# Inverses by logarithm and exponential, eight-largest routing, and eight maxima steps ahead in a two-layer kernel

## Time and profile before

| | |
|---|---|
| median of three runs | 3710.39 us |
| profiled execution, its span | 3709.09 us, 3707.4 us |
| busy: TensorE, VectorE, ScalarE, GpSimd | 81%, 67%, 56%, 35% |
| mean granted TensorE clock | 0.906 |
| 655 to 721 us, with the first combining stage | VectorE busy 43.1 us, TensorE 14.3 |
| 721 to 798 us, with routing | VectorE busy 57.7 us, TensorE 10.6 |
| 1088 to 1630 us, with the second attention | TensorE 454.0, VectorE 401.6, ScalarE 317.4, GpSimd 297.3 |
| 1630 to 1691 us, with the second combining stage | VectorE busy 38.8 us, TensorE 8.6 |
| 1691 to 3707 us, transformer blocks and the end | TensorE 1827.7, VectorE 1302.2 |

### The profile page before, as it was taken

The page is one execution under the profiler, slowest core; times in us unless marked ns, Lnnn a source line. Parts: engine busy times, 40 slices in busy tenths (PEclk is TensorE's granted clock), DMA queues, the critical chain, the costliest instruction groups (busy, mean ns, idle before and its releaser), DMA issues. The chain is left out here.

```text
span 3707.4 us, 71470 instructions
## 1 busy us (share of the span) xinstructions
PE 2992.1 (81%) x22883; PEld 1620.1 (44%) x22883; DVE 2466.2 (67%) x4021; ACT 2083.8 (56%) x3805; POOL 1285.4 (35%) x1223
## 2 busy tenths in 40 slices
PE   2688887239738888845999999999999999999997
PEld 1332332113312223313665565566556556655653
DVE  6788888562347777765666666666666666666664
ACT  1477677112204666633666666666666666666664
POOL 0000000004323556624553354345435434544540
PEclk6588789569957999977999999999999999999998
DMA  5221121114231111232111111111111111111111
GB/s 197 84 85 55 62 73 60 56 45 108 67 38 30 35 34 34 37 68 99 38 54 31 49 54 31 42 45 51 34 49 49 35 42 45 49 31 53 38 35 42
DMA packets 195211, 200.31 MB, mean 54 GB/s; under 512 B 119077, under 2 KB 125877, under 8 KB 190090
## 3 DMA queue, kind: packets, MB, share of 16 engines
q1 hardware_dynamic: 193778, 195.46, 19.2%
q10 hardware_dynamic: 1080, 0.25, 0.0%
HBM read 99.84 MB, written 29.46 MB: 35 GB/s over the span
## 5 line engine op out<-in xcount | busy, mean ns | idle before, releaser
L2421 POOL TENSOR_TENSOR tr_t<-tr_t 128x512 f32<-128x512 f32 x384 | 489.7, 1275 | 683.5 <-DVE tr_t L2259 683.5
L2428 POOL TENSOR_TENSOR tr_nq<-tr_t,tr_rn 128x512 f32<-128x512 f32 x384 | 392.2, 1042 | 366.5 <-ACT tr_rn L2155 362.7
L1638 DVE TENSOR_REDUCE attn_mp<-attn_ps 128x1 f32<-128x512 f32 (+3 forms) x664 | 397.3, 656 | 146.4 <-PE attn_ps L1498 76.5
L2258 DVE TENSOR_TENSOR tr_t<-tr_ps,tr_tab 128x512 f32<-128x512 f32 x384 | 263.2, 685 | 241.1 <-ACT tr_sq L2129 241.1
L1957 PE MATMUL tr_ps<-tr_w,tr_xs 128*128 128x512 f32 x768 | 372.5, 607 | 25.0 <-DVE tr_xs L2292 21.8
L684 DVE TENSOR_REDUCE attn_mcol<-attn_ps 128x1 f32<-128x512 f32 x548 | 357.3, 681 | 50.2 <-PE attn_ps L529 40.4
L1600 ACT ACTIVATE attn_pr<-attn_ps 128x768 f32<-128x768 f32 (+2 forms) x352 | 294.9, 868 | 142.3 <-PE attn_ps L1521 140.0
L2143 ACT ACTIVATE tr_rd<-tr_ps 128x384 f32<-128x384 f32 x264 | 129.0, 489 | 376.1 <-PE tr_ps L1976 375.9
L1943 PEld LDWEIGHTS tr_ps<-tr_qT,tr_kT 64*128 64x128 f32 x4224 | 258.5, 188 | 176.6 <-issue 174.9
L1943 PE MATMUL tr_ps<-tr_qT,tr_kT 64*128 64x96 f32 (+1 forms) x4224 | 301.2, 282 | 31.4 <-ACT tr_kT L2164 20.1
L668 ACT ACTIVATE attn_pr<-attn_ps 128x512 f32<-128x512 f32 x512 | 272.6, 600 | 87.1 <-DVE attn_ps L706 68.9
(11 more groups left out here) (257 smaller groups left out, 5177.0 us busy)
## 6 DMA issues: line engine op xcount, KB each, us to landing
tr_v<-tr_va SPq DMA_DIRECT2D x144, 192.0 KB, 2.6
attn_ka<-scratch_kp SPq DMA_DIRECT2D x72, 294.0 KB
tr_v<-tr_va SPq DMA_DIRECT2D x144, 128.0 KB, 2.2
moe_cb<-scratch_combineT SPq DMA_DIRECT2D x32, 512.0 KB
tr_w<-in_w_half SPq DMA_DIRECT2D x12, 1024.0 KB
tr_v<-tr_va SPq DMA_DIRECT2D x48, 256.0 KB, 2.4
scratch_kp<-proj_parts SPq DMA_DIRECT2D x36, 256.0 KB
attn_km<-scratch_kp SPq DMA_DIRECT2D x72, 98.0 KB
```

What stands on the lines that cost most here:

```text
L1638: dve.tensor_reduce(dst, src, AX.X, ALU.max).then_inc(maxed, 1)
L2258: dve.tensor_tensor(out[0], product, table[0], ALU.mult)
L2421: pool.tensor_tensor(t12[:, slot, i, 0, :], t12[:, slot, i, 0, :], t12[:, slot, i, 1, :], ALU.add).then_inc(summed, 1)
L2428: pool.tensor_tensor(nq[:, slot, i, :].rearrange("p (h e) -> p h e", e=DH), t12[:, slot, i, 0, :].rearrange("p (h e) -> p h e", e=DH), rn[ ...
```

## The change

In both combining stages ScalarE makes the softmax inverses, as exp(-ln(den)), one batch entry at a time; the table set that holds both functions is loaded at the stage's start. The sigmoid of the gate becomes an exponential on ScalarE and an addition and a small reciprocal on VectorE. The loads are put in order of batch entry, and VectorE and TensorE go by chunks or batch entries in place of the whole width. In the first stage `1 - gate` is multiplied into `mblk`. The global denominators are still inverted on VectorE. In routing the ranking of 32 experts is replaced by one eight-largest instruction (`dve.max`) per tile, one `match_replace` per tile, which writes -3e38 over those eight, and a comparison with the unchanged values; before it 0.0 is added to all values. The ranking of the groups stays. In the second attention `LEAD_STEPS` goes from 10 to 8, and the negated maxima are made behind unit 16.

```diff
@@ stage_combine0 @@
+            for dst, src in ((mrep, d["mrep"]), (z, d["z"]), (blk, d["headblk"])):
+                sp.dma_start(dst[:], src).then_inc(weights, 16)
+            sp.dma_start(gate[:, 0:1], d["alpha"].partition_broadcast(P)).then_inc(weights, 16)
             for b in range(B):
                 rows = d["o0"][b * H0:(b + 1) * H0, :, :]
-                sp.dma_start(num[:, b * S:(b + 1) * S], rows[:, 0:HD, :]).then_inc(sums, 16)
                 sp.dma_start(den[:, b * S:(b + 1) * S],
-                             rows[:, HD:HD + 1, :].broadcast_to((H0, HD, S))).then_inc(sums, 16)
-            for dst, src in ((wo, d["woT"]), (bo, d["bo"]), (mrep, d["mrep"]), (z, d["z"]), (blk, d["headblk"])):
+                             rows[:, HD:HD + 1, :].broadcast_to((H0, HD, S))).then_inc(sums[b], 16)
+                sp.dma_start(num[:, b * S:(b + 1) * S], rows[:, 0:HD, :]).then_inc(sums[b], 16)
+            for dst, src in ((wo, d["woT"]), (bo, d["bo"])):
                 sp.dma_start(dst[:], src).then_inc(weights, 16)
...
         def _(act):
-            act.wait_ge(weights, 16 * 6)
-            act.activation(gate[:, 1:2], gate[:, 0:1], ACT.Sigmoid).then_inc(gate_ready, 1)
+            act.preload_act_table_set("natural_log_exp_and_others")
             act.wait_ge(neg_ready, 1)
             act.activation(neg[:], neg[:], ACT.Exp).then_inc(exp_ready, 1)
+            act.wait_ge(weights, 16 * 6)
+            act.activation(gate[:, 3:4], gate[:, 0:1], ACT.Exp, scale=-1.0).then_inc(gate_ready, 1)
+            for b in range(B):
+                cols = slice(b * S, (b + 1) * S)
+                act.wait_ge(sums[b], 32)
+                act.activation(den[:, cols], den[:, cols], ACT.Ln).then_inc(den_log, 1)
+                act.wait_ge(den_log, b + 1)
+                act.activation(den[:, cols], den[:, cols], ACT.Exp, scale=-1.0).then_inc(den_ready, 1)
...
-                pe.matmul(ps[:, c, :], mblk[:], sig[:, c * CH:(c + 1) * CH], start=True, stop=True)
-                mm = pe.matmul(ps[:, 4 + c, :], zblk[:], sig[:, c * CH:(c + 1) * CH], start=True, stop=True)
-            mm.then_inc(glob, 1)
-            pe.wait_ge(mixed, 1)
+                pe.matmul(ps[:, 4 + c, :], zblk[:], sig[:, c * CH:(c + 1) * CH], start=True, stop=True)
+                pe.matmul(ps[:, c, :], mblk[:], sig[:, c * CH:(c + 1) * CH], start=True, stop=True).then_inc(glob, 1)
             for c in range(NC):
+                pe.wait_ge(mixed, c + 1)
...
-            dve.wait_ge(sums, 16 * 4)
-            link(dve.reciprocal(den[:], den[:]))
-            link(dve.tensor_tensor(num[:], num[:], den[:], ALU.mult))
-            dve.wait_ge(glob, 1)
+            dve.scalar_tensor_tensor(mblk[:], mrep[:], gate[:, 2:3], blk[:], ALU.mult,
+                                     ALU.mult).then_inc(blocks_ready, 1)
             for c in range(NC):
-                g = glob_den[:, c * CH:(c + 1) * CH]
+                cols = slice(c * CH, (c + 1) * CH)
+                g = glob_den[:, cols]
+                dve.wait_ge(glob, c + 1)
                 link(dve.tensor_scalar(g, ps[:, 4 + c, :], 1e-6, None, ALU.add))
                 link(dve.reciprocal(g, g))
                 link(dve.tensor_tensor(g, g, ps[:, c, :], ALU.mult))
-            link(dve.tensor_scalar(glob_den[:], glob_den[:], gate[:, 2:3], None, ALU.mult))
-            dve.scalar_tensor_tensor(num[:], num[:], gate[:, 1:2], glob_den[:], ALU.mult,
-                                     ALU.add).then_inc(mixed, 1)
+                dve.wait_ge(den_ready, c // 2 + 1)
+                link(dve.tensor_tensor(num[:, cols], num[:, cols], den[:, cols], ALU.mult))
+                dve.scalar_tensor_tensor(num[:, cols], num[:, cols], gate[:, 1:2], g, ALU.mult,
+                                         ALU.add).then_inc(mixed, 1)
@@ stage_route @@
-            rank(sc, E_, pick[:])
-            link(dve.tensor_scalar(pick[:], pick[:], TOP_K - 0.5, None, ALU.is_lt))
+            link(dve.tensor_scalar(sc[:], sc[:], 0.0, None, ALU.add))
+            for n in range(NT):
+                last = dve.max(best[:, n, :], sc[:, n, :])
+            link(last)
+            for n in range(NT):
+                last = dve.match_replace(left[:, n, :], best[:, n, :], sc[:, n, :], -3.0e38)
+            link(last)
+            link(dve.tensor_tensor(pick[:], left[:], sc[:], ALU.not_equal))
@@ stage_attention1 @@
-LEAD_STEPS = 10
+LEAD_STEPS = 8
...
-                        if a == 14:
+                        elif a == 16:
                             negate_rows(kv + 1, (s + 1) % 2, kv)
@@ stage_combine1 @@
+            for b in range(B):
+                for j in range(2):
                     rows = d["o1"][OROW + b * NQ1:OROW + (b + 1) * NQ1].rearrange("(n j) r s -> j n r s", j=2)[j]
+                    sp.dma_start(den[j][:, b * S:(b + 1) * S],
+                                 rows[:, HD:HD + 1, :].broadcast_to((NQ1 // 2, HD, S))).then_inc(sums[b], 16)
+                    sp.dma_start(num[j][:, b * S:(b + 1) * S], rows[:, 0:HD, :]).then_inc(sums[b], 16)
+                if b == 0:
+                    for j in range(4):
+                        sp.dma_start(lam[:, j, :], d["lam"][j].partition_broadcast(P)).then_inc(weights, 16)
+                    sp.dma_start(wp[:], d["wproj"]).then_inc(weights, 16)
...
+            for b in range(B):
+                cols = slice(b * S, (b + 1) * S)
+                act.wait_ge(sums[b], 64)
+                for j in range(2):
+                    act.activation(den[j][:, cols], den[j][:, cols], ACT.Ln).then_inc(den_log, 1)
+                for j in range(2):
+                    act.wait_ge(den_log, 2 * b + j + 1)
+                    act.activation(den[j][:, cols], den[j][:, cols], ACT.Exp, scale=-1.0).then_inc(den_ready, 1)
+                if b == 0:
+                    act.wait_ge(lam_sum, 1)
+                    act.activation(lsum[:, 0:2], lsum[:, 0:2], ACT.Exp).then_inc(lam_exp, 1)
...
-            pe.wait_ge(mixed, 4)
             for b in range(B):
+                pe.wait_ge(mixed, 2 * b + 2)
...
-                link(dve.reciprocal(den[j][:], den[j][:]))
-                link(dve.tensor_tensor(num[j][:], num[j][:], den[j][:], ALU.mult))
-            link(dve.scalar_tensor_tensor(num[0][:], num[1][:], lsum[:, 3:4], num[0][:], ALU.mult, ALU.add))
+                for j in range(2):
+                    dve.wait_ge(den_ready, 2 * b + j + 1)
+                    link(dve.tensor_tensor(num[j][:, cols], num[j][:, cols], den[j][:, cols], ALU.mult))
+                link(dve.scalar_tensor_tensor(num[0][:, cols], num[1][:, cols], lsum[:, 3:4], num[0][:, cols],
+                                              ALU.mult, ALU.add))
```

More of the change, by code:

```diff
@@ L741, in stage_combine0 @@
         mblk, zblk = st.sb("mblk", [P, P]), st.sb("zblk", [P, P])
-        gate = st.sb("gate", [P, 3])
+        gate = st.sb("gate", [P, 4])
         sig, neg = st.sb("sig", [P, T]), st.sb("neg", [P, T])
         ps = st.ps("ps", [P, 8, CH])
-        weights, sums, chain = st.sem("weights"), st.sem("sums"), st.sem("chain")
+        weights, chain = st.sem("weights"), st.sem("chain")
+        sums = [st.sem("sums0"), st.sem("sums1")]
+        den_log, den_ready = st.sem("den_log"), st.sem("den_ready")
         q_back, x_back = st.sem("q_back"), st.sem("x_back")
@@ L829, in stage_route @@
         grp, gsel, t8 = st.sb("grp", [P, NT, EG]), st.sb("gsel", [P, NT, EG]), st.sb("t8", [P, NT, EG])
-        cmp_ = st.sb("cmp", [P, NT, E_, E_])
+        cmp_ = st.sb("cmp", [P, NT, EG, EG])
+        best, left = st.sb("best", [P, NT, TOP_K]), st.sb("left", [P, NT, E_])
         tot = st.sb("tot", [P, NT])
@@ L881, in _ @@
                     link(dve.tensor_tensor(grp[:], grp[:], t8[:], ALU.max))
-            def rank(vals, K, out):
-                for other in range(K):
-                    for lo, hi, op in ((0, other + 1, ALU.is_gt), (other + 1, K, ALU.is_ge)):
-                        if hi > lo:
-                            last = dve.tensor_tensor(cmp_[:, :, lo:hi, other],
-                                                     vals[:, :, other:other + 1].broadcast_to((P, NT, hi - lo)),
-                                                     vals[:, :, lo:hi], op)
-                link(last)
-                link(dve.tensor_reduce(out, cmp_[:, :, 0:K, 0:K], AX.X, ALU.add))
-            rank(grp, EG, t8[:])
+            for other in range(EG):
+                for lo, hi, op in ((0, other + 1, ALU.is_gt), (other + 1, EG, ALU.is_ge)):
+                    if hi > lo:
+                        last = dve.tensor_tensor(cmp_[:, :, lo:hi, other],
+                                                 grp[:, :, other:other + 1].broadcast_to((P, NT, hi - lo)),
+                                                 grp[:, :, lo:hi], op)
+            link(last)
+            link(dve.tensor_reduce(t8[:], cmp_[:], AX.X, ALU.add))
             link(dve.tensor_scalar(gsel[:], t8[:], TOP_GROUPS - 0.5, None, ALU.is_lt))
```

(22 more changed lines are left out.)

17 lines of the change are left out of this document (9 added, 8 removed).

## The result

The changed kernel took 3623.81 us (median of 4 runs, 3620.31 to 3629.77) against 3711.01 before: a ratio of 0.9766, 95% interval 0.9751 to 0.9781. The forecast was 3632, with a range of 3616 to 3656. The span of the profiled execution is 3622.7 us.

A forecast was written before the change was run, and what follows sets the result against it. No engine is busy throughout; stages stand one behind the other, each with its own bound, SP's queue in the second attention. Terms -14.8, -38.6, -20.6 and -4.5 sum to -78.5, giving 3632 us, range 3616 to 3656.

The forecast's parts named there:

- TensorE bounds after all: Rival, second attention: SP's chain starts earlier, up to 1 us per group comes back; 3614 to 3624 us, chance 0.14.
- First combining, -14.8: First combining stage: long reciprocal and plain order go, small loads' arrival stays; ends at 706.0, not 720.80, 14.8 us less.
- Routing, -38.6: Routing: 45.8 us of comparisons and reduction go, not_equal and 32 MAX and MATCH_REPLACE come; 38.6 us less.
- Second combining, -20.6: Second combining stage: ends at 1669.7, not 1690.26, with the transfer late next, no longer VectorE; 20.6 us less.
- Second attention, -4.5: Second attention: gains only ahead of the loop and at its turns, groups staying bound by SP's queue; 4.5 us less.
- Ahead of the loop two steps less are taken: -2.7: Second attention, before its loop: two maxima steps move into the groups, under the SP chain; 2.7 us less.
- at the three turns of the loop it counts: -1.8: Second attention, three loop turns: TensorE 0.6 us earlier at a group's end counts there; 1.8 us less.
- Cold starts: Rival, second attention: longer waits at group starts bring the low clock; 3645 to 3668 us, chance 0.20.
- Dear eight-largest operations: Rival, routing: the eight-largest operations take 1 us each, 32 in place of 6.5; 3657 us, chance 0.06.
- Rows too late: Rival, second attention: rows ready after SP comes for them, so every group grows; 3745 us at ten units, chance 0.02.

The follow-up runs named there:

- first_split: Changed kernel with a separate semaphore for the output weights and bias loads of the first combining stage; 3605.61 us, ratio 0.9715.
- second_only: Kernel before the change with only the new second combining stage put in; 3685.86 us, ratio 0.9942.
- den_shared: Changed kernel whose second combining stage loads only the first map's denominators and uses them for both maps (result differs); 3616.25 us, ratio 0.9750.
- rows_first: Changed kernel with the row transfer moved ahead of a group's second store in SP's list in the second attention; 3589.76 us, ratio 0.9674.
- rows_first_lead10: rows_first with LEAD_STEPS at 10 again and the negation behind unit 14, as before the change; 3614.59 us, ratio 0.9739.
- route_only: Kernel before the change with only the new routing put in; 3666.78 us, ratio 0.9888.
- attn_only: Kernel before the change with only the second attention's eight steps ahead and negation behind unit 16; 3696.28 us, ratio 0.9964.
- lead6: rows_first with LEAD_STEPS at 6 in place of 8 and the negation behind unit 19 in place of 16; 3616.49 us, ratio 0.9754.

## Why the prediction was right, and where it was not

**The sum.** The changed kernel's median lies 8 us below the forecast and inside its range. In the pair of profiles the four terms measured -15.4, -40.8, -22.7 and -5.4, together -84.3 of the 84.7 us between the two profiled executions; the forecast was -78.5, each term a little too small. The time alone would not have told the forecast from the rival *TensorE bounds after all*, whose range of 3614 to 3624 it also meets; the traces do.

**First combining, -14.8.** Right: the stage took 66.1 to 67.0 in four profiles without the new stage and 50.9 to 52.4 in the six with it unaltered, 14.8 less on average. The arrival left at 671, the start of the chunks (678.10, predicted 677.8), their 6.22 (6.35) and the end (705.93, predicted 706.0) are as worked out. first_split showed what held the start. One reading was wrong without touching the sum: beside the long reciprocal TensorE was at work too, with its products for the global term, from 676.43 to 685.5.

**Routing, -38.6.** Right in kind, 2.2 too small: 40.8 by stage length. The 32 operations cost 4.3 us and not 6.5, less than my lower bound of 4.9. They overlap: a MAX has a mean duration of 0.177 us, and the next one starts 0.09 us after it. The estimate of 9.1 by the rule in the Trainium skill, "VectorE: DVE Perf Modes", section "The DRAIN you can't avoid", was the farthest off. The prediction left out the section's exception, that a next operation starts earlier where it is not held; the trace agrees with the exception, by these 0.09 against 0.177 us.

**Second combining, -20.6.** Right, 2 too small in this pair: the first half landed 12.1 and not 12.6 us after the issue, the second 21.1 and not 21.6, and from VectorE's last scaling (1599.28) TensorE and ScalarE needed 7.7 us in place of the 9.2 that I left standing. That last part varies: it took 9.0 in second_only and 8.4 on average over the nine profiles with the new stage and all its loads. By the average stage lengths, 60.3 before (four profiles) and 38.0 (those nine), the term is -22.2. That the transfer bounds the stage is shown by den_shared.

**Second attention, -4.5.** The profile pair alone shows 5.4, but that agreement is luck; over the nine profiles of the table the mean is 11.5. The mechanism (SP's queue bounds the plain groups, so they gain nothing) is shown by rows_first and by the plain groups' sums. Two parts of the term were mis-sized. "Ahead of the loop two steps less are taken: -2.7" measured 4.5, though the steps themselves were 3.0 (from the row issue to a unit's first product: 10.0 before, 7.0 now); the rest lies between that product and the first copy. And "at the three turns of the loop it counts: -1.8", which is 0.6 per turn, measured 5.4; why a turn gains 1.8 is not shown. A plain group that SP's queue does not bound became 0.84 shorter (rows_first_lead10 against rows_first), not 0.6. The rows came 20.0 us after the group's start instead of 19.0 (1225.40 against 1206.38 in the earlier trace rows), one us later and not 2.6.

**The rivals.** *Cold starts*: partly true. There were nine spells of the low clock where there were five (44 us against 27 in the profiles). What they cost wasn't measured by itself, but the sum of the plain groups stayed, and the 3645 us and more did not come. The clock of 1.00 at the groups' starts, as forecast, was not there in nine of them, and the waits were not 1 to 2 us but 0.3 to 3.1. In the changed kernel's profile waits of 1.94 us and more at a group's start were followed by the low clock and shorter ones were not; over all nine profiles waits between 1.7 and 2.0 us went either way (1.78 in route_only was followed by it, 1.99 in attn_only was not). The Trainium skill's "TensorE: Matmul & The Clock Gate", section "HAM oscillation — how this bites in real kernels", describes a kernel in which transfer waits of 3 to 5 us made every burst start cold; the trace agrees for the waits of that length, and shows cold starts behind waits of 2 us as well. *TensorE bounds after all*: refuted for the change, because its waits for the row transfer grew. *Dear eight-largest operations*: refuted, by 4.3 us for all of them. *Rows too late*: doesn't occur here; lead6 shows where it begins.

## What to carry to other kernels

Ask of each stage what is late next, and of a queue that serves loads, stores and one urgent transfer, in what order it serves them: moving four DMA issues ahead of four others was worth 34 us here, three times what the edit of TensorE's order brought by itself (11.5), and it raised that edit's worth to 25. One counting semaphore for several loads makes everything wait for the last of them; taking two late ones out of it was worth 7.0 us of the stage. And compare a small term over several profiles before trusting one pair.

## What the runs showed that was not expected

- VectorE's operations on 128x32 follow each other closer than they last: MAX 0.09 apart at 0.177, MATCH_VALUE_LOAD with MATCH_REPLACE8 0.16 apart at 0.08 and 0.18.
- A turn of this attention's loop (four groups written out) costs about 4 us (31.1 against 27.1 in rows_first). For 2.9 to 3.1 of it TensorE waits for nothing that the profile shows; in each of the three the low clock followed. That fetching the code is the cause is not shown.
- The same code ahead of the first combining stage took 651.1 to 660.6 us in different profiles, a difference larger than several of the terms argued over here.
- The low clock comes and goes in the second combining stage as well: the same work behind VectorE's last scaling took 7.7 us at a granted clock of 0.79 and 9.0 at 0.67.
